# Adjacency loads as entries of SyncE's list, with new lists and bank assignments for all engines

## The chip, the core and the metric

The kernel runs on one core of a Trainium2 chip. Its time is the device time of one execution in microseconds, and the figure that counts is the median of the runs. One more execution was taken with the hardware profiler; all rows below come from that one.

## What is computed

The input `x` has 8 batches of 1024 nodes with 128 features, `adj` is one 1024 x 1024 int32 adjacency matrix for all of them. Two layers follow each other, each with a LayerNorm and a ReLU ahead of it and the input added behind it:

```python
h = relu(layernorm(x))
q, k, v = h @ Wq.T + bq, h @ Wk.T + bk, h @ Wv.T + bv        # 4 heads of 32
scores = clip(q k.T / sqrt(32), -10, 10), -10 where adj == 0
ctx = sum over 8 chunks of 128 keys: softmax within the chunk @ v
x = x + layernorm(ctx @ Wo.T + bo + h) * gamma + beta
h = relu(layernorm(x))
wh = h @ W;  e = leaky_relu(wh @ a1 + (wh @ a2).T, 0.2), -inf where no edge
x = x + elu(softmax(e) @ wh)
```

## The kernel before

Each batch is handled in two halves of 512 nodes. The first layer has 16 steps for a batch (2 halves of queries by 8 chunks of keys). A step has four heads in two groups: TensorE multiplies stacked queries and keys into PSUM (`scores`, 32 groups for a batch), ScalarE takes the exponential in place (`exp`), and VectorE clips it between a floor and a mask table called `cap` and writes it to SBUF (`probs`). TensorE then makes the sums (`sums`) and the weighted values (`context`), ScalarE inverts the sums by a logarithm and an exponential (`log_sum`, `inverse`), VectorE multiplies, and GpSimd adds up the chunks (`gather`). The second layer runs one to two batches behind, woven into the same engines: `peaks`, `leaky`, `hide`, `gat_exp`, `share`.

The order of work is written out as data. For each engine there is a table (`TENSOR`, `SCALAR`, `VECTOR`, `GPSIMD`, `SYNC`) that gives, for each batch and each kind of work, a number for each piece. `in_order(engine)` sorts the pieces by `b * PLACES + place`, and each engine's program runs through that list. An engine executes in order, so a piece that waits for a semaphore holds up all that stands behind it. `BANKS` says which of four PSUM banks each piece of work gets. The numbers only rank; nothing waits for a time.

All loads and stores except seven small ones are issued by SyncE (SP in the rows), from one list and onto one queue:

- `load_x` brings a half of a batch into `x_in`. It waits until TensorE has turned the half before (`turn_x`) and until that half's normalized form has been stored (`h_stored`).
- `store_h` keeps the normalized half in DRAM (`h_kept`), `load_residual` brings it back into `res` together with `x` into `h1`.
- `stack_key` and `stack_query` spread the keys and queries of a half over four head positions: four copies of 256 KB each from `parts` (the first batch's keys from `ring`) into `key_stack` and `query_stack`. The `scores` wait for them. ScalarE may write the next query half into `parts` only once the last copy out of it is complete.

The adjacency matrix comes in eight row tiles of 512 KB (`adj_raw(t)`): tiles 0 to 3 into `probs`, 4 and 5 into `ring`, 6 into `base_row`, 7 into `scratch`. ScalarE casts the even tiles and VectorE the odd ones (`cast`), TensorE turns each (`mask`, eight 128x128 transposes), ScalarE copies the turned tile (`mask` in its list), and VectorE makes three tables out of it (`edges`: three `tensor_scalar`). The first `probs` need the tables of tiles 0 to 3; those of the second half of the queries need all eight. In the kernel before, SyncE issues all eight tiles and the six small loads of the second layer's weights and rows (`rest_loaded`) ahead of its list.

Of the kernel before, what the change touches and what calls it, by code (L numbers as in the profile page):

```python
# [14 lines left out]
P = 128  # L15
# [37 lines left out]
        "turn_x": [912, 1814],  # L53
        "key": [1056, 2292],
        "mask": [1151, 1205, 1434, 1516, 1910, 2238, 2510, 3784],
        "value": [1259, 2564],
        "query": [1348, 2424],
        "bias_row": [2001],
        "scores": [2192, 2378, 2653, 2742, 2981, 3078, 3317, 3430, 3685, 3838, 4048, 4205, 4390, 4559, 4935, 5150,
            5267, 5522, 5674, 5836, 5998, 6171, 6420, 6565, 6891, 7053, 7304, 7365, 7612, 7726, 7969, 8110],  # L60
        "weights": [2703, 3884],
        "sums": [2797, 3133, 3485, 4260, 4462, 4710, 5322, 5577, 6063, 6236, 6620, 6956, 7420, 7785, 8165, 8489],
        "context": [2884, 3220, 3935, 4623, 4838, 5000, 5739, 5900, 6323, 6707, 6794, 7207, 7508, 7872, 8252, 8576],
        "project": [6476, 9429],
        "turn_hidden": [9785, 13357],
        "to_row": [10380, 13580],
        "wh": [13138, 15636, 15865],
        "near_row": [16884, 18776],
        "base_row": [16937, 17036],
        "share": [19450, 19684, 20157, 20382, 22900, 23079, 24071, 24339],  # L70
    },
    1: {
        "turn_x": [-5860, -4503],
        "query": [-5481, -735],
        "key": [-4181, -1576],
        "value": [-2492, -871],
        "scores": [-1251, -1166, -927, -782, -544, -294, -217, 33, 344, 400, 734, 866, 1136, 1297, 1546, 1659, 1894,
            2035, 2274, 2436, 2598, 2759, 3020, 3172, 3482, 3605, 3828, 4103, 4255, 4533, 4665, 4904],
        "sums": [-641, -391, 88, 542, 921, 1362, 1781, 2090, 2501, 2824, 3324, 3660, 4158, 4807, 5035, 5284],
        "context": [-479, 247, 455, 1008, 1200, 1449, 2177, 2339, 2662, 3075, 3237, 3883, 4720, 5122, 5445, 5532],  # L80
        "project": [2921, 8082],
        "turn_hidden": [7655, 12501],
        "to_row": [12254, 13182],
        "wh": [14268, 15156, 15327],
        "base_row": [15651, 15794],
        "near_row": [15704, 17611],
        "share": [17727, 17905, 18780, 19252, 20899, 21209, 21434, 21726],
    },
    2: {
        "turn_x": [-11517, -9681],  # L90
        "query": [-8961, -5021],
        "key": [-7651, -5200],
        "value": [-5289, -3710],
        "scores": [-4620, -4381, -4219, -3971, -3809, -3620, -3390, -3260, -3021, -2880, -2639, -2478, -2210, -2097,
            -1858, -1680, -1419, -1180, -898, -719, -480, -274, -90, 89, 438, 663, 902, 1136, 1364, 1603, 1665,
            2105],
        "sums": [-3906, -3487, -2824, -2737, -2042, -1803, -1115, -1011, -577, -203, 153, 805, 1506, 1807, 2008,
            2804],
        "context": [-3205, -3118, -2575, -2413, -1615, -1364, -1277, -664, -371, -26, 718, 1419, 1720, 2395, 2557,
            3124],  # L100
        "project": [2161, 7334],
        "turn_hidden": [6532, 10211],
        "to_row": [10125, 11477],
        "wh": [12058, 12304, 12523],
        "base_row": [13212, 14826],
        "near_row": [13266, 15196],
        "share": [16060, 16239, 16961, 17294, 18832, 19173, 20029, 20253],
    },
    3: {
        "turn_x": [-14711, -13354],  # L110
        "query": [-12565, -6150],
        "key": [-10442, -7696],
        "scores": [-7349, -7108, -6851, -6645, -6531, -6205, -6064, -5543, -5497, -4988, -4775, -4551, -4283, -3967,
            -3919, -3453, -3363, -3124, -2832, -2776, -2451, -2312, -1897, -1645, -1519, -1116, -964, -715, -467,
            -136, 5, 230],
        "value": [-7303, -4865],
        "sums": [-6389, -5442, -5268, -5085, -4228, -3733, -3308, -3016, -2548, -2168, -1829, -1061, -812, -233,
            372, 802],
        "context": [-6302, -5355, -5181, -4141, -3646, -3221, -2929, -2635, -2081, -1994, -1742, -899, 285, 715,
            963, 1211],  # L120
        "project": [-646, 4165],
        "turn_hidden": [5447, 8417],
        "to_row": [8170, 9100],
        "wh": [10361, 10878, 11237],
        "base_row": [12004, 12097],
        "near_row": [12053, 14187],
        "share": [14298, 14477, 14931, 15119, 16988, 17272, 17460, 17798],
    },
    4: {
        "turn_x": [-16199, -14105],  # L130
        "query": [-13428, -8540],
# [78 lines left out]
}  # L210
SCALAR = {
    0: {
        "apply_x": [743, 1645],
        "first_weights": [897],
        "turn_x": [992, 2121],
        "cast": [1039, 1314, 1799, 2169],
# [1603 lines left out]
```

## Time and profile before

| | |
|---|---|
| median of 3 runs | 697.75 us (696.25 to 698.24) |
| profiled execution | 700.85 us, of which its span is 698.9 us |
| TensorE busy | 650.5 us, 93% of the span |
| VectorE busy | 652.1 us, 93% |
| ScalarE busy | 644.2 us, 92% |
| GpSimd busy | 495.4 us, 71% |
| mean granted TensorE clock | 0.979 |

A row of the timeline gives start, duration, engine, line and what is written from what, and in brackets how long the engine had been idle before it and what ended that. `DVE` is VectorE, `ACT` ScalarE, `PE` TensorE, `POOL` GpSimd; `SPq` are SyncE's DMA issues, whose duration is that of the issue and not of the transfer.

### The profile page before, as it was taken

The numbers are of one execution on the slowest core, as the hardware profiler recorded it, in microseconds if no ns is written. First come the engines' busy times: TensorE is split into PE (matmuls) and PEld (weight loads), VectorE is DVE, ScalarE is ACT, GpSimd is POOL, SyncE is SP. The second block draws the span as 40 slices with busy tenths as digits, with TensorE's granted clock in tenths as the row PEclk, the third lists the DMA queues.
The fourth block names the chain that finished last, engine by engine and source line by source line (L and its number), as shares of the span: only waits on it lengthen the run. The fifth ranks groups of instructions, "written<-read, shape, count | busy, mean of one in ns | idle before, by whom it ended". The sixth has DMA issues, their size and how long they took to land.

```text
span 698.9 us, 13786 instructions
## 1 busy us (share of the span) xinstructions
PE 650.5 (93%) x4393; PEld 345.9 (49%) x4393; DVE 652.1 (93%) x1285; ACT 644.2 (92%) x1128; POOL 495.4 (71%) x637
## 2 busy tenths in 40 slices
PE   4588999999999999999999999999999999997695
PEld 3332333343336474556445564547446573456595
DVE  3689999999999999999999999999999999999785
ACT  5789999998999999999999999999999999994866
POOL 2014669643596866987688758888388769999886
PEclk9799999999999999999999999999999999999699
DMA  8554043115033152232042134131431224010023
GB/s 284 183 196 136 1 151 137 61 60 196 1 122 106 58 185 74 94 120 96 28 151 76 59 102 151 51 124 40 151 113 62 76 77 144 23 45 32 0 64 89
DMA packets 58647, 68.53 MB, mean 98 GB/s; under 512 B 5328, under 2 KB 35024, under 8 KB 58576
## 3 DMA queue, kind: packets, MB, share of 16 engines
q1 hardware_dynamic: 57568, 67.39, 28.4%
q8 instruction: 36, 0.59, 0.3%
q10 hardware_dynamic: 1008, 0.26, 0.2%
q14 instruction: 35, 0.29, 0.1%
HBM read 21.50 MB, written 12.58 MB: 49 GB/s over the span
## 4 chain that ended last, share of the span: by engine, by line
PE 52%; ACT 18%; DVE 11%; DMA 6%; issue 6%; POOL 3%; SPq 3%; POOLq 0%; DVEq 0%; ACTq 0%
PE score L1678 12%; PE work L1762 10%; PE work L1695 10%; PE work L1689 10%; ACT score L1328 6%; DVE probs L1479 5%; PE work L1649 3%; PE work L1705 2%; ACT ring L1394 2%; DVE ring L1573 2%; ACT inverse L1335 2%; PE work L1740 2%; ACT inverse L1338 2%; SPq L1123 2%; PE work L1732 1%
## 5 line engine op out<-in xcount | busy, mean ns | idle before, releaser
L1479 DVE SCALAR_TENSOR_TENSOR probs<-score,cap 128x1024 f32<-128x1024 f32 x256 | 307.8, 1216 | 10.1 <-ACT score L1328 8.2
L1328 ACT ACTIVATE score<-score 128x1024 f32<-128x1024 f32 x256 | 259.6, 1023 | 8.3 <-PE score L1678 6.7
L1678 PE MATMUL score<-query_stack,key_stack 128*128 128x512 f32 x512 | 189.6, 456 | 12.4 <-DVE probs L1479 7.0
L1248 POOL TENSOR_TENSOR gathered<-gathered,scaled 128x512 f32<-128x512 f32 x112 | 143.9, 1285 | 45.0 <-DVE scaled L1505 43.2
L1678 PEld LDWEIGHTS score<-query_stack,key_stack 128*128 128x128 f32 x512 | 79.9, 190 | 137.6 <-DVE probs L1479 85.5
L1280 POOL TENSOR_TENSOR ring<-ring,see_t 128x512 f32<-128x512 f32 x120 | 139.7, 1180 | 9.2 <-DVE ring L1573 9.0
L1695 PE MATMUL work<-probs,ones 128*32 128x512 f32 x1024 | 135.1, 601 | 3.1 <-ACT inverse L1335 1.1
L1689 PE MATMUL work<-probs,value 128*32 128x512 f32 x1024 | 134.0, 602 | 2.5 <-DVE scaled L1505 1.9
L1762 PEld LDWEIGHTS work<-wh,ring 128*128 128x128 f32 x896 | 105.2, 190 | 10.8 <-DVE gathered L1505 2.7
L1762 PE MATMUL work<-wh,ring 128*128 128x130 f32 x896 | 108.3, 276 | 0.3 <-ACT ring L1394 0.2
L1394 ACT ACTIVATE ring<-ring,wh 128x512 f32<-128x512 f32 x128 | 89.6, 725 | 0.4 <-POOL ring L1280 0.2
L1338 ACT ACTIVATE inverse<-inverse 128x512 f32<-128x512 f32 x128 | 80.9, 638 | 0.3
L1335 ACT ACTIVATE inverse<-work 128x512 f32<-128x512 f32 x128 | 76.7, 602 | 3.8 <-DVE scaled L1505 2.3
L1505 DVE TENSOR_TENSOR scaled<-work,inverse 128x512 f32<-128x512 f32 x112 | 76.3, 683 | 2.7 <-ACT inverse L1338 1.1
L1573 DVE SCALAR_TENSOR_TENSOR ring<-work,wh,base_row 128x512 f32<-128x512 f32 x96 | 69.5, 742 | 0.2
L1203 POOL TENSOR_TENSOR small<-small,eps 128x4 f32<-128x4 f32 x48 | 9.7, 202 | 74.0 <-DVE small L1460 73.8
L1689 PEld LDWEIGHTS work<-probs,value 128*32 128x32 f32 x1024 | 24.8, 108 | 63.0 <-issue 32.5
L1695 PEld LDWEIGHTS work<-probs,ones 128*32 128x32 f32 x1024 | 23.6, 108 | 59.2 <-issue 29.5
L1206 POOL TENSOR_TENSOR small<-small,minus_half 128x4 f32<-128x4 f32 x48 | 48.9, 1019 | 3.8
L1705 PE MATMUL work<-h_t,w_t 128*128 128x512 f32 x64 | 36.3, 651 | 0.7 <-ACT h_t L1346 0.7
L1236 POOL TENSOR_TENSOR res<-res,rows 128x512 f32<-128x512 f32 x16 | 20.5, 1281 | 20.7 <-ACT res L1316 20.7
L1551 DVE CUSTOM_DVE_ANT_0 scratch<-work,see,peak 128x512 f32<-128x512 f32 x48 | 34.4, 743 | 0.0
(118 smaller groups left out, 848.1 us busy)
## 6 DMA issues: line engine op xcount, KB each, us to landing
query_stack<-parts SPq DMA_DIRECT2D x64, 256.0 KB, 3.0
key_stack<-parts SPq DMA_DIRECT2D x56, 256.0 KB, 2.6
x_in<-in_x SPq DMA_DIRECT2D x16, 256.0 KB, 2.9
h_kept<-x_in SPq DMA_DIRECT2D x16, 256.0 KB, 3.1
res<-h_kept SPq DMA_DIRECT2D x16, 256.0 KB, 2.8
h<-in_x SPq DMA_DIRECT2D x16, 256.0 KB, 3.2
x_kept<-res SPq DMA_DIRECT2D x16, 256.0 KB, 2.6
gat_x<-x_kept SPq DMA_DIRECT2D x32, 128.0 KB, 2.4
```

Source lines behind the costliest of these rows:

```text
L1248: nc.gpsimd.tensor_tensor(sums, sums, scaled[:, k % SCALED], ALU.add).then_inc(gathered_step, 1)
L1280: nc.gpsimd.tensor_tensor(ring[:, k, :], ring[:, k, :], see_t[:, k % CHUNKS, side], ALU.add).then_inc(hidden_done, 1)
L1328: nc.scalar.activation(some, some, ACT.Exp, bias=RAISED, scale=DH ** -0.5).then_inc(exp_done, 1)
L1335: nc.scalar.activation(inverse[:, k % LOGS], work[:, bank, :], ACT.Ln).then_inc(work_read[bank], 1)
L1338: nc.scalar.activation(inverse[:, k % LOGS], inverse[:, k % LOGS], ACT.Exp, scale=-1.0).then_inc(share_ready, 1)
L1394: nc.scalar.activation(ring[:, k, :], ring[:, k, :], ACT.Exp, bias=ends(b)[:, k % CHUNKS, 3:4]).then_inc(gat_exp_done, 1)
L1479: nc.vector.scalar_tensor_tensor(out=probs[:, group_of(b, k) % KEPT], in0=score[:, h:h + GROUP, :], scalar=LOW, in1=caps.broadcast_to([P, ...
L1573: nc.vector.scalar_tensor_tensor(out=ring[:, k, :], in0=row, scalar=ends(b)[:, j, 2:3], in1=base_row[:, side], op0=ALU.add, op1=ALU.max).t ...
L1678: last = nc.tensor.matmul(score[:, head, :], key_stack[:, head, chunk * P:(chunk + 1) * P], query_stack[:, head, half * HALF:(half + 1) * ...
L1689: last = nc.tensor.matmul(work[h * DH:(h + 1) * DH, bank, :], value[:, chunk, h * DH:(h + 1) * DH], of_head(b, k, h), start=True, stop=True)
L1695: last = nc.tensor.matmul(work[h * DH:(h + 1) * DH, bank, :], ones[:, :], of_head(b, k, h), start=True, stop=True)
L1762: last = nc.tensor.matmul(work[:, bank, part * (SIGNS + D):(part + 1) * (SIGNS + D)], ring[:, half * CHUNKS + jt, k % TILES * P:(k % TILES ...
```

## The change

The eight adjacency loads and the six small loads are no longer ahead of SyncE's list but entries of it (`load_adj`, `load_rest`), and all five tables of places and the bank string have new numbers. No piece of work is added or removed on any other engine, and none is changed.

```diff
@@ SYNC, batch 0
-        "store_h": [1306, 1986],
-        "stack_key": [1349, 2846],
-        "stack_query": [1736, 3181],
-        "load_residual": [3096, 4780],
+        "load_adj": [546, 589, 632, 675, 718, 956, 1239, 1947],
+        "store_h": [913, 1990],
+        "load_rest": [999],
+        "stack_key": [1317, 2834],
+        "stack_query": [1612, 3830],
+        "load_residual": [1862, 2704],
@@ program of SyncE
             for q in (0, 1):
                 sp.wait_ge(x_loaded[q], 16)
-            for t in range(CHUNKS):
-                sp.dma_start(adj_raw(t), adj_tile[t]).then_inc(adj_loaded[t], 16)
-            sp.dma_start(w1[:, 0:D], W).then_inc(rest_loaded, 16)
-            for e in (0, 1):
-                sp.dma_start(a_in[:, e:e + 1], a[e * D:(e + 1) * D, :]).then_inc(rest_loaded, 16)
-            for n, b in enumerate((bo, gamma, beta)):
-                row = b.rearrange("(o f) -> o f", o=1).broadcast_to([P, D])
-                sp.dma_start(rows[:, n, :], row).then_inc(rest_loaded, 16)
+
+            def load_rest():
+                sp.dma_start(w1[:, 0:D], W).then_inc(rest_loaded, 16)
+                for e in (0, 1):
+                    sp.dma_start(a_in[:, e:e + 1], a[e * D:(e + 1) * D, :]).then_inc(rest_loaded, 16)
+                for n, b in enumerate((bo, gamma, beta)):
+                    row = b.rearrange("(o f) -> o f", o=1).broadcast_to([P, D])
+                    sp.dma_start(rows[:, n, :], row).then_inc(rest_loaded, 16)
...
             for name, k, b in in_order("sync"):
-                if name == "load_x":
+                if name == "load_adj":
+                    sp.dma_start(adj_raw(k), adj_tile[k]).then_inc(adj_loaded[k], 16)
+                elif name == "load_rest":
+                    load_rest()
+                elif name == "load_x":
```

SyncE's issues at the start, between the adjacency tiles and the first stacked queries. Before (`probs` took tiles 0 to 3 ahead of this; `w` to `rows` are the six small loads, `h_kept<-x_in` is `store_h` of half 0, `x_in<-in_x` is `load_x` of half 0 of batch 1):

```order
L1113 DMA ring<-in_adj 128x1024 x2
L1113 DMA base_row<-in_adj 128x1024
L1113 DMA scratch<-in_adj 128x1024
L1114 DMA w<-in_L_gnn_W 128x128
L1116 DMA a_in<-in_L_gnn_a 128x1 x2
L1119 DMA rows<-in_L_gnn_bo 128x128
L1119 DMA rows<-in_L_gnn_gamma 128x128
L1119 DMA rows<-in_L_gnn_beta 128x128
L1141 DMA h_kept<-x_in 128x512
L1123 DMA key_stack<-ring 32x4x512 x4
L1138 DMA x_in<-in_x 128x4x128
L1123 DMA query_stack<-parts 32x4x512 x4
```

The same stretch of SyncE now:

```order
L1135 DMA ring<-in_adj 128x1024
L1146 DMA h_kept<-x_in 128x512
L1135 DMA ring<-in_adj 128x1024
L1115 DMA w<-in_L_gnn_W 128x128
L1117 DMA a_in<-in_L_gnn_a 128x1 x2
L1120 DMA rows<-in_L_gnn_bo 128x128
L1120 DMA rows<-in_L_gnn_gamma 128x128
L1120 DMA rows<-in_L_gnn_beta 128x128
L1135 DMA base_row<-in_adj 128x1024
L1124 DMA key_stack<-ring 32x4x512 x4
L1143 DMA x_in<-in_x 128x4x128
L1124 DMA query_stack<-parts 32x4x512 x4
```

The store of the first half went ahead of tile 5, the small loads ahead of tile 6, and tile 7 (`scratch`) left the stretch. Tiles 5 and 6 still stand ahead of the stacked keys.

What follows on SyncE. Before:

```order
L1141 DMA h_kept<-x_in 128x512
L1123 DMA key_stack<-ring 32x4x512 x4
L1155 DMA res<-h_kept 128x512
L1156 DMA h<-in_x 128x4x128
L1123 DMA query_stack<-parts 32x4x512 x4
L1138 DMA x_in<-in_x 128x4x128
L1141 DMA h_kept<-x_in 128x512
L1138 DMA x_in<-in_x 128x4x128
```

Now (the last `x_in<-in_x` of these rows is half 0 of batch 2, and the last row the stacking of the second query half of batch 0):

```order
L1160 DMA res<-h_kept 128x512
L1161 DMA h<-in_x 128x4x128
L1135 DMA scratch<-in_adj 128x1024
L1146 DMA h_kept<-x_in 128x512
L1160 DMA res<-h_kept 128x512
L1161 DMA h<-in_x 128x4x128
L1143 DMA x_in<-in_x 128x4x128
L1124 DMA key_stack<-ring 32x4x512 x4
L1146 DMA h_kept<-x_in 128x512
L1143 DMA x_in<-in_x 128x4x128
L1124 DMA query_stack<-parts 32x4x512 x4
```

Both residual loads and tile 7 now stand ahead of the second key stacking, the load of half 1 of batch 1 (`x_in`) too, and the second query stacking has gone behind a store and a load of the next batches.

TensorE around the first scores (`work<-ring` are the turned tiles, eight transposes each; L1705, now L1710, is a query or key product, L1649, now L1654, a value product). Before:

```order
L1644 MATMUL work<-eye,x_in 128x128 x4
L1787 MATMUL work<-ring 128x128 x8
L1745 MATMUL work<-w_t,bias_v 128x128
L1678 MATMUL score<-query_stack,key_stack 128x512 x2
L1787 MATMUL work<-ring 128x128 x8
L1705 MATMUL work<-h_t,w_t 128x512
L1678 MATMUL score<-query_stack,key_stack 128x512 x2
L1705 MATMUL work<-h_t,w_t 128x512
L1787 MATMUL work<-ring 128x128 x8
L1649 MATMUL work<-w_t,h_t 128x128 x4
L1678 MATMUL score<-query_stack,key_stack 128x512 x2
```

Now:

```order
L1649 MATMUL work<-eye,x_in 128x128 x4
L1792 MATMUL work<-ring 128x128 x8
L1710 MATMUL work<-h_t,w_t 128x512
L1654 MATMUL work<-w_t,h_t 128x128 x4
L1683 MATMUL score<-query_stack,key_stack 128x512 x4
L1798 MATMUL work<-eye,w 128x128
L1792 MATMUL work<-ring 128x128 x8
L1710 MATMUL work<-h_t,w_t 128x512
L1683 MATMUL score<-query_stack,key_stack 128x512 x4
```

The sixth tile, the second half's keys and its values went from between the first groups of scores to ahead of them, and the first two groups stand next to each other.

## Rows read from the trace of the kernel before

**Rows 1.** The page, part 1: busy us, share of the span, instructions.

```profile
PE 650.5 (93%) x4393; PEld 345.9 (49%) x4393; DVE 652.1 (93%) x1285; ACT 644.2 (92%) x1128; POOL 495.4 (71%) x637
```

**Rows 2.** Stretches: us, busy by engine, granted clock, DMA share, GB/s.

```profile
20.00:30.00 10.00, 4.98 (x25) 3.26 (x26) 5.18 (x17) 6.39 (x8) 0.00 (x0) 0.57 0.74 270
...
60.00:600.00 540.00, 529.64 (x3568) 263.12 (x3568) 529.24 (x1002) 527.52 (x902) 399.16 (x496) 1.00 0.28 96
```

**Rows 3.** Chain of work that ended last, first 70 us: start, us, what.

```profile
12.66 8.28 DMA h_kept<-x_in
...
23.30 3.86 DMA query_stack<-parts
27.20 1.22 PE score L1678 x2
...
41.83 4.84 DMA x_in<-in_x
```

**Rows 4.** Timeline of SyncE's issues.

```profile
14.72 2.67 SPq L1123 DMA_DIRECT2D key_stack<-ring  x4
21.00 0.39 SPq L1138 DMA_DIRECT2D x_in<-in_x  x1
21.43 3.09 SPq L1123 DMA_DIRECT2D query_stack<-parts  x4
...
35.12 2.49 SPq L1123 DMA_DIRECT2D key_stack<-ring  x4
...
38.89 2.84 SPq L1123 DMA_DIRECT2D query_stack<-parts  x4
```

**Rows 5.** DMA view of the issues at 7.1 and at 41 us: last number us to landing.

```profile
probs<-in_adj SPq DMA_DIRECT2D x1, 512.0 KB, 6.9
...
query_stack<-parts SPq DMA_DIRECT2D x1, 256.0 KB, 5.2
```

**Rows 6.** Shorter stretches, with columns as in rows 2.

```profile
18.00:19.00 1.00, 0.00 (x0) 0.00 (x0) 1.00 (x4) 1.00 (x3) 0.00 (x0) 1.00 0.57 124
...
21.00:24.00 3.00, 1.55 (x10) 1.02 (x10) 0.00 (x0) 2.80 (x4) 0.00 (x0) 0.56 1.08 378
24.00:27.20 3.20, 0.00 (x0) 0.00 (x0) 2.64 (x9) 0.73 (x1) 0.00 (x0) 0.50 0.96 355
```

**Rows 7.** Timeline of ScalarE.

```profile
18.30 1.67 ACT L1316 ACTIVATE x_in<-x_in,small 128x128 f32<-128x128 f32 x4
...
28.46 1.01 ACT L1328 ACTIVATE score<-score 128x1024 f32<-128x1024 f32 x1 [0.94 <-PE score L1678]
...
31.90 1.01 ACT L1328 ACTIVATE score<-score 128x1024 f32<-128x1024 f32 x1 [1.50 <-PE score L1678]
...
34.76 1.96 ACT L1328 ACTIVATE score<-score 128x1024 f32<-128x1024 f32 x2
...
52.45 0.69 ACT L1352 ACTIVATE parts<-work,bias_col 128x512 fp32r<-128x512 f32 x1 [0.51 <-PE work L1705]
```

**Rows 8.** Timeline of VectorE.

```profile
35.85 2.36 DVE L1479 SCALAR_TENSOR_TENSOR probs<-score,cap 128x1024 f32<-128x1024 f32 x2 [0.75 <-ACT score L1328]
...
46.70 0.87 DVE L1453 BATCH_NORM_STATS2 small<-x_in 128x6 f32<-128x128 f32 x4 [1.39 <-DMA x_in<-in_x]
...
52.07 1.23 DVE L1479 SCALAR_TENSOR_TENSOR probs<-score,cap 128x1024 f32<-128x1024 f32 x1 [0.61 <-ACT score L1328]
...
54.08 1.23 DVE L1479 SCALAR_TENSOR_TENSOR probs<-score,cap 128x1024 f32<-128x1024 f32 x1 [0.50 <-ACT score L1328]
...
56.82 1.51 DVE L1627 TENSOR_SCALAR see_t<-ring 128x1024 bf16<-128x1024 bf16 x1
```

**Rows 9.** Timeline of GpSimd.

```profile
55.33 2.71 POOL L1248 TENSOR_TENSOR gathered<-gathered,scaled 128x512 f32<-128x512 f32 x2
```

**Rows 10.** Waits from 60 to 600 us, of VectorE, then ScalarE: us, times, longest.

```profile
DVE probs L1479 <- ACT score L1328: 3.9, 12, 0.8
...
ACT parts L1352 <- DMA key_stack<-parts: 2.2, 2, 1.2
```

More of the change, by code:

```diff
@@ L52 @@
     0: {
[L53 to L70, printed above, removed]
-    },
-    1: {
[L73 to L87, printed above, removed]
-    },
@@ L89 @@
-    2: {
[L90 to L107, printed above, removed]
-    },
@@ L109 @@
-    3: {
[L110 to L127, printed above, removed]
-    },
@@ L189 @@
[L189 to L208 removed]
+        "turn_x": [912, 1928],
@@ new lines @@
+        "key": [1056, 2071],
+        "mask": [1151, 1205, 1577, 1671, 1837, 2017, 2492, 3809],
+        "bias_row": [1259],
+        "query": [1316, 2546],
+        "value": [1402, 2249],
+        "scores": [2380, 2426, 2678, 2791, 3032, 3116, 3355, 3468, 3763, 3863, 4086, 4249, 4428, 4679, 4818, 5189,
+            5353, 5560, 5714, 5878, 6130, 6210, 6454, 6600, 6841, 6920, 7255, 7401, 7642, 7746, 7987, 8129],
+        "weights": [2472, 4229],
+        "sums": [2847, 3172, 3524, 4304, 4494, 5091, 5255, 5616, 6032, 6265, 6743, 7062, 7457, 7802, 8272, 8498],
@@ L212 @@
     0: {
[L213 removed]
+        "apply_x": [743, 1571],
         "first_weights": [897],
[L215 to L222 removed]
@@ new lines @@
+        "turn_x": [992, 1999],
+        "cast": [1039, 1314, 1725, 2047],
+        "key": [1165, 2231],
+        "mask": [1224, 1482, 1820, 1910, 2142, 2288, 2632, 4070],
+        "query": [1425, 3003],
+        "value": [2378, 2722],
+        "exp": [2446, 2539, 2769, 2862, 3112, 3205, 3452, 3545, 3829, 3930, 4163, 4370, 4540, 4839, 4980, 5326,
+            5430, 5627, 5824, 5969, 6219, 6312, 6556, 6667, 6961, 7106, 7401, 7494, 7734, 7827, 8067, 8196],
+        "log_sum": [2955, 3638, 3767, 4463, 4932, 5523, 5571, 5922, 6171, 6405, 6914, 7199, 7587, 7968, 8397, 8633],
@@ L684 @@
[L684 to L697 removed]
+        "rstd_x": [551, 1211],
@@ new lines @@
+    6: {
+        "load_x": [-23878, -22443],
+        "store_h": [-18924, -16114],
+        "stack_query": [-14632, -9779],
+        "stack_key": [-13399, -11418],
+        "load_residual": [-7570, -4731],
+        "store_x1": [-1974, 982],
+        "load_x1": [6787, 7175, 7333, 7836],
+        "store_out": [7526, 7793, 8072, 8350],
+    },
+    7: {
+        "load_x": [-27148, -25410],
+        "stack_query": [-17962, -11867],
+        "stack_key": [-16110, -14581],
+        "store_h": [-13686, -11489],
+        "load_residual": [-11152, -7638],
+        "store_x1": [-2616, -2031],
+        "load_x1": [-1618, -1339, -1061, -661],
+        "store_out": [-868, -704, -351, -273],
```

1170 lines of the change are left out of this document (602 added, 568 removed).

## The prediction, made before the run

> **What bounds the kernel now.** I read the page first: VectorE, TensorE and ScalarE are each busy for 92 or 93% of the span [rows 1], so no engine stands alone as the bound. The table of stretches then says where the other 7% lie. From 60 to 600 us all three are busy for 527 to 530 of 540 us, about 98% [rows 2]; nothing but a shorter instruction or less work could bring much there. From 20 to 30 us they are busy for about 5 of 10 us, and TensorE's granted clock falls to 0.57, towards the lower of its two levels, 1.2 GHz, where it lies near 0.5 in the last stretch before the first scores [rows 2, 6]. So the start is the place.
>
> The chain of waits names what is late there. A 256 KB store, `h_kept<-x_in`, is issued at 12.66 us and takes 8.28 us to complete [rows 3]. SyncE has issued the first stacked keys from 14.72 to 17.39 us, and then stands still: its next entry, `load_x` of the next batch, waits for that store and is issued at 21.00 us. The stacked queries stand behind it and are issued from 21.43 to 24.52 us [rows 4]. Their last copy lands at 23.30 + 3.86 = 27.16 us, and the first scores start at 27.20 us [rows 3]. The store was slow because eight adjacency tiles and the small loads stood ahead of it on the same queue: tile 4, issued at about 7.2 us, needed 6.9 us itself [rows 5].
>
> There is a second place. `load_x` of half 1 of the next batch is issued at 41.83 us, behind the second query stacking, and needs 4.84 us [rows 3]; VectorE's statistics wait 1.39 us for it, and two `probs` after them idle 0.61 and 0.50 us [rows 8].
>
> **The change, part by part.** The durations are those of the profiled execution (700.85 us; span 698.9 us and 1.95 us around it), 3.1 us above the median of the runs. I take the gain off its 700.85 us and carry the same difference over to the median, 697.75 us.
>
> *A. The first scores.* The store of half 0 now stands behind five tiles. Tile 4 landed at 7.2 + 6.9 = 14.1 us [rows 5], and 256 KB at 378 GB/s are 0.7 us [rows 6], so it is complete at about 15 us and `load_x` finds no wait at 17.4 us. The query stacking can then be issued at 17.8 us, 3.6 us sooner. It doesn't gain all of that, since the queue is full: the DMA share is 1.08 from 21 to 24 us and 0.96 until 27.2 us [rows 6]. What the queue saves is tile 7, 512 KB at 378 GB/s, 1.4 us, and a part of the slack from 17 to 20 us, where the share fell to 0.57 [rows 6]. That is 1.4 us at least and 2.3 at most, and the first scores should start at about 25.6 us.
>
> *B. The second group of scores.* Until now the sixth tile and a product stand between the first two groups of scores on TensorE, at the lower clock; ScalarE's first exponential starts at 28.46 us and the second only at 31.90 us, after 1.50 us of idling, the third at 34.76 us [rows 7]. In the new order these are done ahead of the scores, in the time in which the engines waited for the DMA. I count what ScalarE then has ahead of its first exponential: `apply_x` of half 1 ends at about 19.2 us (one mask copy of about 0.9 us fewer ahead of it than at its 18.30 + 1.67 us before [rows 7]); behind it come two casts and four mask copies at 0.9 to 1.0 us, a key at 0.6, and two copies at 0.5 us, 7.2 us, which ends at 26.4 us. The first scores end at 25.6 + 1.2 = 26.8 us, so ScalarE isn't late. The second exponential follows at about 28.2 us, then a mask and a value copy of 1.5 us together, and the third and fourth exponentials start at about 31 and 32 us. The pair of `probs` that VectorE ended at 35.85 + 2.36 = 38.2 us [rows 8] would end at about 34.4 us. A and B together bring 3.8 us. The floor is A's 1.4 us, if the pulled-up work doesn't fit ahead of the scores; the most is 4.5 us, what ScalarE and VectorE could close up here.
>
> *C. The second load.* `load_x` of half 1 now stands ahead of the second key stacking, some 10 us sooner. The wait of 1.39 us is gone, and with it the 0.61 and 0.50 us behind it, since they come from scores that TensorE ran late after that stall [rows 8]: 2.5 us. The lower bound is 1.4 us.
>
> *D. A wait that is new.* SyncE now stands before the second query stacking with a `store_h` and the `load_x` of batch 2 behind it. The load waits for the turning of half 0 of batch 1, about 41 us in the new order, so the stacking is issued from about 41.5 to 44.4 us, and not from 38.89 us [rows 4] less 3.8 us. The second half's scores need it only near 59 us. But ScalarE writes the next batch's first queries into `parts`, and waits for the last copy out of it; that copy took 5.2 us in the trace [rows 5] with other loads around it, and about 3.9 us without, so it lands between 47.5 and 49 us. ScalarE reached these queries at 52.45 us [rows 7], and with the gain so far would reach them at 46.5 to 47 us. Behind them stand the next exponentials, and VectorE's half of the queries with the `probs` behind it. VectorE gets there at about 47.5 us by its own work, so the loss is about 1.0 us, nothing at best and 2.5 us at worst. In the same way half 1's store is late behind the first query stacking, and `load_residual` and the second key stacking behind it; those keys land near 36 us and are wanted near 40, so this costs nothing, and up to 1 us if the queue is 5 us later.
>
> *E. GpSimd next to VectorE's mask tables.* One of them took 1.51 us in place of some 0.4 while GpSimd ran two additions for 2.71 us [rows 8, 9]. GpSimd's `residual` and both `beta` additions of batch 0 now stand earlier, in the stretch where such tables are made. By the rows this is 0 to 1.1 us for an encounter; I take 0, since the tables before the first `probs` have time to spare and the later ones met additions before too. The Trainium skill, "SBUF — State Buffer", on the ports, says that the pair of ports that VectorE and GpSimd share is an exclusive lock, so that the loser stands still for the whole instruction. By that rule E is a loss of up to one addition, some 1.3 us, for each encounter, and the sum would be 1.3 us higher with one more; the stretched table agrees with it, and how often the new order lets them meet no row can tell.
>
> *F. All the rest of the lists.* The same work in nearly the same order, most pieces within five places of where they stood. VectorE's `probs` wait for only 3.9 us in all from 60 to 600 us [rows 10], and the three engines idle 10 to 12 us each [rows 2]. So new lists can't bring much; they can lose a little in each batch. I take 0, within 2.5 us either way.
>
> The sum is 3.8 + 2.5 - 1.0 = 5.3 us. The profiled execution would take 695.5 us, the median 697.75 - 5.3 = 692.4 us. The shift should last to the end, since behind 60 us no engine has room to absorb it or to make it up.
>
> **The rivals.** *Only the queue's bytes count.* The DMA queue is full until 27.2 us [rows 6], for which A alone speaks, 1.4 us; the work pulled ahead of the first exponential then arrives late, and C and D cancel. The median is 696.4 us. Against it stands that engines idled for half of this time [rows 2]. Chance 0.11.
>
> *Encounters on GpSimd's side.* By the lock that is named under E, the three additions moved forward could each block VectorE for 1.3 us, 3.9 us in all, which leaves 5.3 - 3.9 = 1.4 us of gain and a median of 696.3 us. One stretched table in the trace speaks for it; against it, that they moved into a stretch in which VectorE mostly runs `probs`. Chance 0.06.
>
> *Slower.* The mechanism of D in the steady state: ScalarE's `parts` waited for key stackings only twice from 60 to 600 us, 1.2 us at the longest [rows 10]. The new list of SyncE has other neighbours around the stackings in every batch. If seven batches each had one such wait of 1.2 us, the loss would be 8.4 us and the median 697.75 - 5.3 + 8.4 = 700.9 us. It decides from (5.3 + 2.1) / 7 = 1.06 us in each batch. Chance 0.11.
>
> *More than the sum.* The stretch from 30 to 60 us closes up fully and F brings its 2.5 us: 4.5 + 2.5 + 2.5 = 9.5 us, and a median of 688.3 us. Chance 0.12.
>
> **How the numbers follow.** The forecast has a chance of 0.60, with its own range of 689.5 to 695.5 us. 0.3%, which is 2.1 us, is about what a measurement of this kernel can tell from no change. Faster by more than that are the forecast and the last rival, 0.72; the first two rivals lie within it, 0.17; slower is 0.11. The range of 8 in 10 takes in the first two rivals and most of the last one: 688.8 to 697.0 us.
>
> **What would show it.** In the changed kernel's profile: `load_x` directly behind the key stacking, at about 17.5 us, the query stacking at 17.8 us, and the first scores near 25.6 us (A); the first two exponentials next to each other, and the fourth `probs` ended by 35 us (B); no wait of the statistics for `x_in` near 42 us (C); a wait of ScalarE's `parts` or VectorE's for the query stacking near 47 us, of 2.5 us at most (D); mask tables of 0.4 us, apart from one or two (E); and from 60 to 600 us the three engines at 98% again (F). The prediction is wrong if the first scores start later than 26.5 us, if D's wait exceeds 4 us because the second query stacking is issued after 45 us, or if the steady stretches fall to 97% or below.

## The result, and the profile after

The changed kernel takes 686.45 us (median; 686.16 to 686.82 in 4 runs), the kernel before took 697.00 us beside it (694.56 to 698.24). The ratio is 0.9853, with an interval of 0.9824 to 0.9883, so it is faster by about 10.3 us. The forecast was 5.3 us and 692.4 us; the range ended at 688.8 us, and the result lies 2.35 us below it.

The page of the changed kernel, first its busy times, then the costliest wait of VectorE's `probs` by group:

```profile
span 684.8 us, 13786 instructions
PE 645.3 (94%) x4393; PEld 344.6 (50%) x4393; DVE 648.5 (95%) x1285; ACT 641.6 (94%) x1128; POOL 496.0 (72%) x637
L1484 DVE SCALAR_TENSOR_TENSOR probs<-score,cap 128x1024 f32<-128x1024 f32 x256 | 307.2, 1216 | 5.8 <-ACT score L1333 4.1
```

Against [rows 1] the span is 14.1 us shorter, but the profiled execution of before was a long one; a second trace of the same kernel (run `x0`, below) has a span of 695.2 us, and I compare with it wherever sizes matter. The stretches of [rows 2] now read:

```profile
20.00:30.00 10.00, 7.09 (x52) 4.39 (x49) 7.94 (x22) 9.32 (x13) 1.18 (x1) 1.00 0.93 332
60.00:600.00 540.00, 533.45 (x3618) 268.45 (x3620) 532.06 (x1010) 529.86 (x912) 404.30 (x501) 1.00 0.28 95
```

From 20 to 30 us the three engines are busy for 7.1, 7.9 and 9.3 us in place of 5.0, 5.2 and 6.4 us, and TensorE's granted clock stays at its full level in this trace, where it was 0.57 (in the second trace of the changed kernel, `y0` below, it falls there too). But from 60 to 600 us each of them is also busy for 2.3 to 3.8 us more of the same 540 us. That is where I had expected nothing.

The timeline of SyncE, to be read against [rows 4]:

```profile
7.27 0.53 SPq L1135 DMA_DIRECT2D ring<-in_adj  x1
9.32 0.33 SPq L1146 DMA_DIRECT2D h_kept<-x_in  x1
...
18.02 0.69 SPq L1143 DMA_DIRECT2D x_in<-in_x  x1
18.76 2.84 SPq L1124 DMA_DIRECT2D query_stack<-parts  x4
...
31.51 0.45 SPq L1143 DMA_DIRECT2D x_in<-in_x  x1
...
42.10 2.62 SPq L1124 DMA_DIRECT2D query_stack<-parts  x4
```

The timeline of the changed kernel: TensorE, ScalarE (first two groups of exponentials, then the `parts` near 47 us) and VectorE, to be read against [rows 3, 7, 8]:

```profile
27.33 1.20 PE L1683 MATMUL score<-query_stack,key_stack 128*128 128x512 f32 x4 [0.68 <-DMA query_stack<-parts]
...
28.10 1.93 ACT L1333 ACTIVATE score<-score 128x1024 f32<-128x1024 f32 x2 [0.68 <-PE score L1683]
31.30 2.11 ACT L1333 ACTIVATE score<-score 128x1024 f32<-128x1024 f32 x2
47.21 0.69 ACT L1357 ACTIVATE parts<-work,bias_col 128x512 fp32r<-128x512 f32 x1 [0.20 <-DMA query_stack<-parts]
...
29.22 2.35 DVE L1484 SCALAR_TENSOR_TENSOR probs<-score,cap 128x1024 f32<-128x1024 f32 x2 [1.40 <-ACT score L1333]
32.39 2.35 DVE L1484 SCALAR_TENSOR_TENSOR probs<-score,cap 128x1024 f32<-128x1024 f32 x2
41.71 0.86 DVE L1458 BATCH_NORM_STATS2 small<-x_in 128x6 f32<-128x128 f32 x4
```

The query stacking is issued 2.7 us sooner than before, and in this pair of traces the scores start no sooner (27.33 us against 27.20). All the same the fourth `probs` ends at 32.39 + 2.35 = 34.7 us, where it ended at 38.2 us: the exponentials come in pairs with no wait between the pairs. The statistics at 41.71 us don't wait for `x_in`.

### The profile page after: what moved, and what is told of

Same layout as the page of the kernel before. It is cut to its first block and busy times, and to the rows that moved or that the text cites. A ratio compares the mean times of both kernels' runs of the same rounds, so it can differ in the third digit from the quotient of the medians.

```text
span 684.8 us, 13786 instructions
## 1 busy us (share of the span) xinstructions
PE 645.3 (94%) x4393; PEld 344.6 (50%) x4393; DVE 648.5 (95%) x1285; ACT 641.6 (94%) x1128; POOL 496.0 (72%) x637
## 5 line engine op out<-in xcount | busy, mean ns | idle before, releaser
L1683 PE MATMUL score<-query_stack,key_stack 128*128 128x512 f32 x512 | 187.7, 451 | 7.4 <-DVE probs L1484 6.2
L1285 POOL TENSOR_TENSOR ring<-ring,see_t 128x512 f32<-128x512 f32 x120 | 140.3, 1182 | 13.6 <-DVE ring L1578 13.4
L1683 PEld LDWEIGHTS score<-query_stack,key_stack 128*128 128x128 f32 x512 | 78.3, 188 | 131.0 <-DVE probs L1484 93.1
L1694 PE MATMUL work<-probs,value 128*32 128x512 f32 x1024 | 132.2, 599 | 0.0
L1710 PE MATMUL work<-h_t,w_t 128*128 128x512 f32 x64 | 35.5, 637 | 0.8 <-ACT h_t L1351 0.7
L1556 DVE CUSTOM_DVE_ANT_0 scratch<-work,see,peak 128x512 f32<-128x512 f32 x48 | 34.7, 742 | 0.2 <-DVE peak L1556 0.2
L1321 ACT ACTIVATE x_in<-x_in,small 128x128 f32<-128x128 f32 x64 | 26.5, 503 | 5.6 <-POOL small L1214 5.6
```

Of the source, the lines that this page charges most:

```text
L1285: nc.gpsimd.tensor_tensor(ring[:, k, :], ring[:, k, :], see_t[:, k % CHUNKS, side], ALU.add).then_inc(hidden_done, 1)
L1683: last = nc.tensor.matmul(score[:, head, :], key_stack[:, head, chunk * P:(chunk + 1) * P], query_stack[:, head, half * HALF:(half + 1) * ...
L1694: last = nc.tensor.matmul(work[h * DH:(h + 1) * DH, bank, :], value[:, chunk, h * DH:(h + 1) * DH], of_head(b, k, h), start=True, stop=True)
```

## Experiments

Sixteen kernels ran. Each ratio is to the kernel before, timed on the same chip beside it. Most of them join the old and new lists, or change numbers of them. The joined ones hold both sets of tables, and take a piece's place from one set up to a turn (the last argument of `joined`, in the tables' own numbers, 9,600 to a batch) and from the other behind it.

### The same kernels again

`x0` is the kernel before and `y0` the changed one, unchanged, for a second trace of each.

> The kernel before, unchanged, as a measure of what two runs of one kernel differ by, and for a second trace of it. If its profiled execution of 700.85 us was an unlucky one, the new one lies near 697 us, the ratio is 1.00, and the new trace shows which of the 3.9 us above the median came from the front, the middle or the tail. If the middle and the tail of the old lists really lose 7 us against the new ones, the new trace shows the same waits at the same places (key stacking near 164 us, TensorE's low clock after 646 us).

> The changed kernel itself, on the same chip as the next three, so that they can be held against it and not only against the kernel before. 686 to 687 us, ratio about 0.985; the same front (first scores near 27.3 us) and the same lower clock from about 635 us.

Measured: 0.9997 (0.9978 to 1.0016) and 0.9856 (0.9829 to 0.9883), with spans of 695.2 and 683.5 us. How VectorE's time divides, by stretch (us, busy of TensorE, its weight loads, VectorE, ScalarE, GpSimd, clock, DMA share, GB/s), first `x0`:

```profile
0.00:60.00 60.00, 39.41 (x233) 19.68 (x237) 40.04 (x95) 44.40 (x71) 13.38 (x39) 0.91 0.60 202
60.00:110.00 50.00, 48.06 (x308) 18.60 (x304) 47.73 (x85) 48.30 (x77) 32.10 (x45) 1.00 0.28 100
110.00:600.00 490.00, 482.70 (x3273) 244.53 (x3272) 481.64 (x918) 479.79 (x827) 367.20 (x454) 1.00 0.29 96
600.00:695.20 95.20, 77.72 (x596) 61.58 (x588) 81.58 (x190) 71.44 (x156) 82.72 (x102) 0.93 0.16 47
```

And `y0`:

```profile
0.00:60.00 60.00, 43.98 (x261) 20.62 (x265) 45.04 (x102) 49.98 (x81) 18.86 (x44) 0.97 0.66 227
60.00:110.00 50.00, 49.86 (x316) 19.78 (x315) 48.65 (x96) 49.34 (x79) 31.88 (x50) 1.00 0.26 92
110.00:600.00 490.00, 484.55 (x3316) 249.02 (x3308) 484.24 (x919) 481.34 (x834) 372.81 (x454) 1.00 0.28 94
600.00:683.50 83.50, 66.50 (x512) 55.08 (x508) 70.56 (x170) 60.75 (x137) 71.83 (x92) 0.96 0.16 48
```

VectorE's idle time is the stretch less its busy time. It falls from 20.0 to 15.0 us until 60 us, from 2.3 to 1.4 until 110, from 8.4 to 5.8 until 600, and from 13.6 to 12.9 behind. That is 5.0 + 0.9 + 2.6 + 0.7 = 9.2 us; its busy time falls by another 2.5 us, from 651.0 to 648.5 (the sums of the two tables). Together they are the 11.7 us between the spans. About half lies in the first 60 us, half behind. The first pair of traces gives 5.0 + 1.2 + 1.6 + 2.7 us by the same stretches: the 5.0 us come back, while the split of what lies behind 60 us is only good to a microsecond or two.

### Which stretch of the lists

`x1` has the new lists until about 97 us, `w4` until about 190, `w2` until 400, and `x3` until 610, each with the old ones behind; `x2` and `w3` are the reverse, with the new lists from 97 and from 620 us on.

```
x1: ENGINES = joined(NEW, OLD, 8970)     x2: ENGINES = joined(OLD, NEW, 8970)
w4: ENGINES = joined(NEW, OLD, 18700)    w2: ENGINES = joined(NEW, OLD, 39875)
x3: ENGINES = joined(NEW, OLD, 60000)    w3: ENGINES = joined(OLD, NEW, 60600)
```

> New lists, banks and adjacency order for the first 100 us or so, the old lists and banks from there on. Theory 1 (the whole gain is made in the start; the rest is luck of one profile): 686 to 688 us, ratio 0.985 to 0.988. Theory 2 (two thirds at the start, one third in the lists behind it): 689 to 690 us, ratio 0.988 to 0.990. Theory 3 (my sum of 5.3 us was right for the start and the other half lies behind it): 691.5 us, ratio 0.992.

> The opposite: old start with the eight adjacency tiles ahead of SyncE's list, new lists and banks from about 100 us on. Theory 1: no difference from before, 696.5 to 697.5 us. Theory 2: 3 to 4 us faster, 693 to 694 us. Theory 3: 5 us faster, 692 us.

> New lists for everything up to about 610 us, the old lists and banks for the last 75 us. The two traces put 3.2 us of the difference into the last 75 us, where TensorE ran at the lower clock for 13.7 us before and 10.2 us now. If the old tail lists cause that, this kernel takes 689 to 690 us. If it is chance of one execution, it takes 686.5 us like the changed kernel.

> New lists and banks until about 195 us, old ones behind. The traces put 7.0 us of the gain ahead of 100 us, 2.6 us between 110 and 600 us, 0.7 us and some busy time behind. If the joint costs nothing, 7 to 8 us faster than before, ratio 0.989. If a joint of lists costs as in the first splices, its loss shows at one place near 195 us and has to be taken off.

> New lists and banks until about 410 us, old ones behind. If the gain of the middle is spread evenly over many small waits, 8 to 9 us faster than before, ratio 0.988, between the run before it and the changed kernel (0.9855). If it sits in the wait at batch 2 and in batches 5 and 6: half and half, the same ratio, but the progress of the probs shows a step.

> Old lists and banks until about 620 us, new ones for the last 70 to 75 us. The counterpart of the third splice. If the new end is better by itself: 1 to 2 us faster than before, ratio 0.9975. If the end only takes what it is given: within 0.5 us of before.

Measured (start in us of a batch's first `probs` and of the very last one, from the traces; then the time of the runs, which were made on three chips, so that the ratios and not the medians should be compared):

| kernel | batch 1 | batch 3 | batch 5 | batch 7 | last `probs` | median us | ratio |
|---|---|---|---|---|---|---|---|
| before (`x0`) | 96.7 | 231.4 | 389.8 | 548.1 | 618.7 | 698.05 | 0.9997 |
| `w4`, new to 190 us | 89.3 | 227.3 | 386.1 | 544.5 | 615.1 | 693.57 | 0.9939 (0.9917 to 0.9961) |
| `w2`, new to 400 us | 89.4 | 223.5 | 380.9 | 541.1 | 611.7 | 691.73 | 0.9918 (0.9892 to 0.9944) |
| `x3`, new to 610 us | 89.8 | 224.0 | 381.4 | 538.7 | 609.6 | 689.77 | 0.9868 (0.9840 to 0.9896) |
| changed (`y0`) | 89.7 | 222.9 | 380.2 | 537.2 | 608.1 | 686.77 | 0.9856 (0.9829 to 0.9883) |
| `w3`, new from 620 us | 96.5 | 231.2 | 389.9 | 547.7 | 618.3 | 696.84 | 0.9980 (0.9965 to 0.9994) |

`x1` came to 0.9975 (0.9959 to 0.9992) and `x2` to 0.9973 (0.9956 to 0.9991), which is no answer to what each part is worth, since a joint itself costs. In `x1` VectorE waits at it longer than anywhere else; its timeline at the joint:

```profile
102.40 1.22 DVE L2264 SCALAR_TENSOR_TENSOR probs<-score,cap 128x1024 f32<-128x1024 f32 x1 [5.24 <-ACT score L2113]
```

`x2` loses 3.8 us at the same place and regains 2.5 us by the end of batch 7. `w4` has 7.4 us of lead at 97 us and 4.1 at 231 us, `w2` 8.9 at 390 us and 7.2 at 471 us. My reading is that the two lists pass the buffers on in different turns, so that a piece comes too late where one ends and the other begins. What these runs do tell, lead by lead: the new lists are 7 us ahead at 97 us and stay so, they gain a further 2.5 to 4 us by 548 us (10.9 us ahead in `y0`, 9.4 in `x3`), and the end alone brings at most 1 or 2 us (`w3`). In `y0` the further lead comes in small steps over five batches. The waits of VectorE from 60 to 600 us, first `x0`:

```profile
DVE probs L1479 <- ACT score L1328: 3.8, 11, 0.9
DVE parts L1487 <- ACT parts L1352: 1.1, 1, 1.1
```

And `y0`:

```profile
DVE probs L1484 <- ACT score L1333: 2.3, 9, 0.4
...
DVE parts L1492 <- ACT parts L1357: 0.3, 1, 0.3
```

### The named change by itself

`y1` undoes in the changed kernel what the change is named for: SyncE issues all eight tiles and the small loads at the start again, with every other list new. `y2` does only that part in the kernel before. `y5` gives the kernel before the whole new list of SyncE for the first 100 us.

```diff
 y1, SyncE's table
-        "load_adj": [546, 589, 632, 675, 718, 956, 1239, 1947],
-        "load_rest": [999],
+        "load_adj": [546, 589, 632, 675, 718, 719, 720, 721],
+        "load_rest": [722],
 y2, in the old lists
+OLD_SYNC[0]["load_adj"] = [500, 501, 502, 503, 504, 1307, 1309, 1900]
+OLD_SYNC[0]["load_rest"] = [1308]
 y5, in the old lists
+OLD["sync"] = joined(NEW, OLD, 8970)["sync"]
```

> All new lists and banks, but SyncE issues the eight tiles and the six small loads ahead of everything, as before. Theory S (the order of SyncE's transfers makes the gain of the start): the store of half 0 is late again, the queries are stacked at 21.4 us, and 4 to 6 us are lost, 691 to 693 us. Theory E (the engines' lists make it, since the work that stood between the first scores went ahead of them, and the transfers were full either way): at most 1.5 us are lost, 686.5 to 688 us.

> All old lists and banks, with one edit: the store of half 0 behind tile 4, then tile 5, the small loads and tile 6, and tile 7 behind the first query stacking. Theory S: 3 to 4 us faster than before, ratio 0.995. Theory E: the first scores start where they did, near 27.3 us, and the time stays within 1 us of before; the statistics' wait for x_in near 24 us is the only thing to shrink.

> Old lists and banks on the four engines, SyncE's whole new list for the first 100 us. Beside the edit of the run before it this also brings the load of half 1 of the next batch ahead of the second key stacking, so my term C (1.4 to 2.5 us) should come on top: Theory S 5 to 6 us faster than before, Theory E about 2 us faster. If the new list of SyncE only fits the new lists of the engines, it is no faster than before, or slower.

Measured: `y1` 0.9839 (0.9815 to 0.9863), 685.8 us; `y2` 1.0011 (0.9994 to 1.0028); `y5` 0.9999 (0.9986 to 1.0013). So the order of the tiles is worth nothing that can be measured, with the new lists (`y1`) or the old ones (`y2`), and in the old lists the whole of SyncE's new list at the start isn't either (`y5`); with the new lists only the tiles and small loads were put back. `y1` is the fastest kernel of all, but its interval overlaps the changed kernel's. Its timeline, of SyncE and then TensorE:

```profile
12.71 0.45 SPq L1146 DMA_DIRECT2D h_kept<-x_in  x1
14.61 2.81 SPq L1124 DMA_DIRECT2D key_stack<-ring  x4
20.34 0.39 SPq L1143 DMA_DIRECT2D x_in<-in_x  x1
20.78 2.71 SPq L1124 DMA_DIRECT2D query_stack<-parts  x4
...
26.61 1.20 PE L1683 MATMUL score<-query_stack,key_stack 128*128 128x512 f32 x4 [1.06 <-DMA query_stack<-parts]
```

SyncE stands still until 20.34 us here, as before, and the first scores still start 0.7 us sooner than in the changed kernel. The first scores start at 27.20 and 28.05 us in the two traces of before, and at 27.33 and 26.89 in those of the changed kernel: 0.5 us between the means, and 0.85 us between two traces of one kernel. The joined kernels give more traces of either start. Over all with the old start (before, `x0`, `x2`, `w3`, `z3`) the queries are issued from 21.43 to 22.55 us and the first scores start from 27.20 to 28.21 us, 27.80 in the mean. Over all with the new start (changed, `y0`, `x1`, `x3`, `w2`, `w4`) it is 18.59 to 18.90 us and 26.28 to 27.33 us, 26.84 in the mean. So the scores did gain about 1.0 us, from queries issued 3.3 us sooner. But `y2` and `y5`, which issue them at 19.09 and 18.74 us in the old lists, start their scores at 27.75 and 27.63 us, like the old start, and `y1`, which issues them at 20.78 us in the new lists, like the new one. The 1.0 us goes with the engines' lists and not with SyncE's; by which of their entries, no run shows.

In `y5` the wait of the statistics for `x_in` was gone, but ScalarE then stood for 0.85 us before its `parts` of the next batch, which is term D; its timeline:

```profile
51.32 0.69 ACT L2139 ACTIVATE parts<-work,bias_col 128x512 fp32r<-128x512 f32 x1 [0.85 <-DMA query_stack<-parts]
```

At 57 us `y5` is level with `x0` again.

### The first two groups of scores

`z1` takes the new lists and moves only the first group back ahead of the sixth tile and the second half's key, where it stood before. `z2` does the opposite in the old lists; `z5` is `z2` with VectorE's first statistics of batch 1 behind them.

```diff
 z1, in the new lists (TensorE, ScalarE, VectorE)
-        "scores": [2380,      "exp": [2446,      "probs": [2551,
+        "scores": [2013,      "exp": [2200,      "probs": [2330,
 z2, in the old lists (TensorE, ScalarE, ScalarE, VectorE)
-        "scores": [2192,      "exp": [2264,      "key": [1165, 2539],      "key": [1237, 2766],
+        "scores": [2377,      "exp": [2445,      "key": [1165, 2400],      "key": [1237, 2435],
 z5, VectorE besides
-        "stats_x": [-7669,
+        "stats_x": [-7315,
```

> The changed kernel with three numbers set back: the first group of scores, its exponential and its probs again ahead of the sixth tile, the second half's keys and values. If the pulled-up work is what the start gained (term B), the second group is late by 2.5 to 3.5 us again and the time is 689 to 690.5 us, ratio 0.990. If the gain of the start is spread over the lists, it is 687 to 688 us, ratio 0.986.

> The kernel before with the same three moved the other way, and the first key product of half 1 on ScalarE and VectorE ahead of them. Term B by itself: 2.5 to 3.5 us faster, ratio 0.996. It can be less, since VectorE still waits 4 to 5 us for the statistics' x_in ahead of the tile that the second keys stand behind: then 0 to 1 us.

> The run before it, and VectorE's statistics of the next batch moved behind the tables of tile 3, so that it doesn't stand waiting for x_in from 20 to 25 us. If the wait is what keeps the pulled-up work back: 3.5 to 4.5 us faster than before, ratio 0.9945, half of what the whole change gives. If it makes no difference: like the run before it.

Measured: `z1` 0.9915 (0.9888 to 0.9942), `z2` 0.9994 (0.9977 to 1.0011), `z5` 0.9971 (0.9952 to 0.9991). Three numbers take 4.2 us off the gain (4.1 us by the ratios). VectorE's timeline in `z1`:

```profile
29.19 1.22 DVE L1484 SCALAR_TENSOR_TENSOR probs<-score,cap 128x1024 f32<-128x1024 f32 x1 [3.93 <-ACT score L1333]
31.48 0.75 DVE L1492 SCALAR_TENSOR_TENSOR ring<-work,bias_col,ring 128x512 fp32r<-128x512 f32 x1 [1.07 <-ACT ring L1357]
...
33.78 1.23 DVE L1484 SCALAR_TENSOR_TENSOR probs<-score,cap 128x1024 f32<-128x1024 f32 x1 [0.55 <-ACT score L1333]
```

And the stretch before it in `z1`:

```profile
24.00:31.00 7.00, 4.20 (x15) 2.64 (x16) 2.42 (x6) 1.35 (x3) 1.26 (x1) 0.52 0.68 241
```

The first `probs` starts at 29.19 us as in the changed kernel (29.22), the second 3.4 us later than there (33.8 against 30.4), and the fourth 3.8 us later (37.3 against 33.5). From 24 to 31 us ScalarE has little to do (1.35 us of 7), TensorE's granted clock falls to 0.52, its lower level, and the tile and the key follow when VectorE and ScalarE should be at scores. TensorE in `z1`:

```profile
26.80 1.22 PE L1683 MATMUL score<-query_stack,key_stack 128*128 128x512 f32 x2 [5.25 <-DMA query_stack<-parts]
27.83 1.08 PE L1792 MATMUL work<-ring 128*128 128x128 bf16 x8
28.70 2.02 PE L1710 MATMUL work<-h_t,w_t 128*128 128x512 f32 x2
...
31.59 0.71 PE L1683 MATMUL score<-query_stack,key_stack 128*128 128x512 f32 x2
...
33.05 0.61 PE L1792 MATMUL work<-ring 128*128 128x128 bf16 x8
33.50 1.08 PE L1710 MATMUL work<-h_t,w_t 128*128 128x512 f32 x2
```

The first three rows are at the lower clock and take 4.32 us, the last three are the same work at the higher one, 2.40 us. So an estimate from these rows is that the clock makes up to 1.9 of the 3.4 us by which the second `probs` is late, and the order of work the rest. That the clock falls isn't special to `z1`: in `y0`, the changed kernel itself, it is at 0.50 from 21 to 24 us, but back by the first scores (0.97 from 24 to 31 us).

```profile
21.00:24.00 3.00, 3.00 (x14) 1.77 (x14) 2.12 (x7) 2.79 (x4) 0.00 (x0) 0.50 1.08 371
```

`z2` shows 2.2 us at the fourth `probs` (35.7 against 37.9 us), is 1.4 us ahead at batch 1 (95.3 against 96.7) and 0.5 us at batch 7 (547.6 against 548.1): the same move that is worth 4.2 us in the new lists is worth nothing that can be measured in the old ones. A part of it goes at the mask tables, the next point: two kinds of them are stretched in `z2` (553 and 552 ns in the mean) where `x0` has one, though the first trace of before also has two. What takes the rest in the old lists stays open. In `z5` the lead lasts; its gain is 2.0 us by the ratio, with an interval of 0.6 to 3.3 us.

### The mask tables beside GpSimd

`z3` moves, in the old lists, one tile's tables behind and one addition of GpSimd ahead, so that they don't meet. `w1` is `z5` and `z3` together: three places of the old lists.

```diff
 z3
-        "edges": [1364, 1514, 1789, 2137, 2299, 3416, 4587, 5254],      "gather": [None, 4611,
+        "edges": [1364, 1514, 1789, 2137, 2299, 3416, 4735, 5254],      "gather": [None, 4080,
```

> The kernel before, with VectorE's three tables of tile 6 moved behind one more probs, and GpSimd's first addition ahead of two small chains, so that tables and additions don't meet (term E). By the traces, which show 1.1 to 1.8 us of stretch there: 1 to 1.5 us faster, ratio 0.998, and all tables at 0.42 us. If the stretch is only moved: no difference, and another table is stretched.

> The kernel before with the edits of the last three runs together: first two groups of scores side by side, the statistics behind the tables of tile 3, tables and additions apart. If the two causes found in the start add up, and the pulled-up scores lost their gain to stretched tables only: 4.0 + 1.3, about 5 us faster than before, ratio 0.992 to 0.993. If something else in the old lists takes it back: 2 to 3 us, ratio 0.996.

Measured: `z3` 0.9980 (0.9962 to 0.9998), `w1` 0.9951 (0.9932 to 0.9969), 693.87 us. One group of VectorE's tables in `x0` (us busy, mean ns of one):

```profile
L1630 DVE TENSOR_SCALAR cap<-ring 128x1024 f16<-128x1024 bf16 x8 | 4.4, 554 | 0.0
```

The place in the timeline of `x0`, VectorE and then GpSimd:

```profile
55.39 0.42 DVE L1627 TENSOR_SCALAR see_t<-ring 128x1024 bf16<-128x1024 bf16 x1
55.72 1.50 DVE L1630 TENSOR_SCALAR cap<-ring 128x1024 f16<-128x1024 bf16 x1
...
55.48 2.88 POOL L1248 TENSOR_TENSOR gathered<-gathered,scaled 128x512 f32<-128x512 f32 x2
```

The same group in `z3`:

```profile
L1630 DVE TENSOR_SCALAR cap<-ring 128x1024 f16<-128x1024 bf16 x8 | 3.3, 418 | 0.0
```

The group in the changed kernel:

```profile
L1635 DVE TENSOR_SCALAR cap<-ring 128x1024 f16<-128x1024 bf16 x8 | 3.4, 421 | 0.0
```

In `z3` the stretched table is gone, as in the changed kernel; what is left are two tables of another kind at 0.54 and 0.52 us. The time of `z3` is 1.4 us less than that of before, with an interval of 0.1 to 2.7 us, so that its size is hardly known.

## Why the prediction was wrong, by its own steps

*Where the kernel is bound.* That from 60 to 600 us "nothing but a shorter instruction or less work could bring much" was the wrong step. 98% of busy time in a stretch of 540 us is still 10.8 us of idling on VectorE [rows 2], and the new lists take some 3.5 us of it (0.9 + 2.6 in the accounts above; 2.8 us in the first pair of traces). I read a high share as an absence of waits. This is where F failed.

*A, the first scores: failed.* The `load_x` at 18.02 us and the query stacking at 18.76 us came as forecast, within 1 us. But the scores started at 27.33 us and not at 25.6, and so behind the 26.5 us that the prediction had named as a sign of being wrong. I had reckoned that tile 7, sent behind the queries, frees its 1.4 us of the queue. By the stretches it didn't: the DMA share of the changed kernel from 21 to 24 us and 24 to 27.2 us, to be read against [rows 6], is as high as before or higher.

```profile
21.00:24.00 3.00, 2.12 (x21) 1.63 (x22) 2.85 (x9) 3.00 (x5) 0.00 (x0) 1.00 1.08 374
24.00:27.20 3.20, 1.93 (x10) 0.97 (x8) 2.69 (x10) 3.20 (x5) 0.00 (x0) 1.00 1.06 371
```

The residual loads and tile 7 are issued at 21.65 to 23.26 us, while the queries are still on their way, and the last two query copies took 5.9 us to land (DMA view), where the last one took 3.9 us before [rows 3]:

```profile
query_stack<-parts SPq DMA_DIRECT2D x2, 256.0 KB, 5.9
```

That later entries take a share of the queue from earlier ones is my reading of this; no run took them away alone. `y1`, which issues its queries 2 us later and isn't any later with its scores, and `y2` and `y5`, which issue them 3 us sooner than the old start and aren't clearly sooner with theirs, say that the issue time isn't what counts here. The first scores gained about 1.0 us over all traces, and not 1.4 to 2.3 us, and the end of the stall on SyncE made no part of it that these runs can show. (The 6.9 us of [rows 5] are also read wrongly there: a row with `probs` is that of tile 3. Tile 4 goes to `ring`, and took 7.8 us. The store found its place all the same.)

The prediction also passed over the longest wait of VectorE in this stretch. Its statistics of the next batch stood ahead of the sixth tile's cast and tables and waited 5.02 us for the `x_in` that SyncE issued behind its stall. In the new list of VectorE they stand behind these tables, and wait 1.05 us (first pair of traces: 4.15 and 0.25 us). The row of `x0`, then that of `y0`:

```profile
25.39 0.87 DVE L1453 BATCH_NORM_STATS2 small<-x_in 128x6 f32<-128x128 f32 x4 [5.02 <-DMA x_in<-in_x]
...
24.16 0.87 DVE L1458 BATCH_NORM_STATS2 small<-x_in 128x6 f32<-128x128 f32 x4 [1.05 <-DMA x_in<-in_x]
```

That is 4 of the 5.0 us by which VectorE idles less until 60 us. The sooner issue didn't do it: `y5` still waits 4.61 us. By the order of the lists this is a part of how B's work got ahead of the scores, but how large a part isn't shown: `z5` moves the statistics alone on top of `z2` and comes to 0.9971 against 0.9994, with intervals that overlap.

*B, the second group: right.* The two groups stand together, ScalarE isn't late, and the fourth `probs` ends at 34.7 us ("by 35 us"). It was forecast at 34.4 us with A and B together worth 3.8 us; the two pairs of traces give 3.5 and 4.8 us, and B carries most of this. `z1` shows it by three numbers: 3.4 us at the second `probs`, 3.8 at the fourth, and 690.93 us against 686.77, 4.2 us, in the time. By the estimate above up to about half is the lower clock during the work that follows the scores there; no run separates the two. And it needs the other new lists around it, since `z2` brings nothing by itself.

*C, the second load: right in kind, its size too large.* The wait of 1.39 us and what followed are gone. But `x0` shows a wait of 1.03 us and nothing behind it, so the 0.61 and 0.50 us that I added came from one execution. `y5` shows that it isn't enough by itself: it comes back as D's wait.

*D, the new wait: over-sized.* It came where it was said, before ScalarE's `parts` at 47.21 us, at 0.20 us and not 1.0.

*E, the mask tables: wrong sign.* The table of 1.51 us [rows 8] beside two additions [rows 9] was there to be removed, and I only asked whether there would be more like it. No table of the changed kernel is stretched. The four kinds of table took 14.4 us in `x0` and 13.5 us in `y0`, 0.9 us less, and 1.8 us less than in the first trace of before. `z3` bears it out by the two numbers that bring it about. The Trainium skill, "SBUF — State Buffer", on the ports, speaks of a lock that stops the loser for the whole instruction. The trace agrees in size: the table lost 1.50 - 0.42 = 1.1 us beside additions of about 1.3 us, and the two additions took 2.88 us beside it, 0.3 us more than two of 1.28.

*F, all the rest: mis-sized.* I took 0 within 2.5 us. Behind 60 us VectorE idles 0.9 + 2.6 + 0.7 = 4.2 us less. This is the term that put the time outside the range.

The sum with measured terms: 5.0 us of idle time on VectorE until 60 us (A to D, forecast 5.3), 4.2 us behind it (F, forecast 0), and 2.5 us of busy time (of which E 0.9, forecast 0), 11.7 us between two traces, and 10.3 us between the medians. Of the 2.5 us of busy time, 1.6 us are spread over many groups at some tenths each, none above 0.4 us; I can't say what makes them. That 5.0 us stand beside a forecast of 5.3 is luck in part: A and C were forecast too large, D's loss too large as well, and the statistics' wait of 4 us was in no term.

*The rivals.* None had it. "More than the sum" was the nearest, with 688.3 us, and its sign and reason (F bringing its full 2.5 us) were right, its size too small. The parts waits of the rival that ended slower came to 1.9 us, once, from 60 to 600 us; the changed kernel's waits of ScalarE:

```profile
ACT parts L1357 <- DMA key_stack<-parts: 1.9, 1, 1.9
```

*What stays open.* Which moves of the middle lists bring its 3 to 4 us. The leads place them between 97 and 548 us, in more than one batch, but the joints of `w4` and `w2` cost 3.3 and 1.7 us themselves, so no single place can be named. For `w1` the gain is less than the 5 us expected of it, and its parts alone sum to 3.4 us (2.0 in `z5`, 1.4 in `z3`). The three places that I understood, put into the old lists (`w1`), bring 3.4 us of the 10.3.

## What to carry to other kernels

Where all engines are about 98% busy, as here, an order laid out anew can still gain by the sum of many small waits. So count the idle microseconds of a stretch, not its share, and bound what new lists can bring by all of them. A large diff's headline need not be its cause: undo the headline alone before explaining it (here `y1`, no slower at all). What is done during an unavoidable wait for a transfer (a tile turned, a key made) was worth 4 us in the new lists and nothing by itself in the old ones, and the moment at which the transfer was issued nothing that could be measured. So look for what stands in the list ahead of owed work and waits, as VectorE's statistics did for 4 to 5 us.

## What the runs showed of the hardware

- With the queue full (DMA share 1.06 to 1.08 in the changed kernel), queries issued some 3 us sooner with the engines' lists unchanged (`y2` and `y5`, 19.09 and 18.74 us against 21.43 to 22.55) were not clearly sooner for the scores: these started at 27.75 and 27.63 us, against 27.20 to 28.21.
- From 21 to 24 us TensorE's granted clock was 1.00 in one trace of the changed kernel and 0.50 in the other (`y0`), and the one with 0.50 started its first scores 0.4 us sooner. In `z1` it was 0.52 from 24 to 31 us, where the scores' own work stood, and eight transposes took 1.08 us in place of 0.61.
- A table on VectorE took 1.50 us in place of 0.42 beside two additions on GpSimd, and these 2.88 us for the two in place of 1.28 each.
- Two lists of the same work, each good as a whole, lost up to 5.2 us in one wait where one was joined to the other.
- The same kernel's first scores lay 0.85 us apart in two traces (27.20 and 28.05 us). A term of less than a microsecond should be read from more than one trace.
